# Residual sums as identity matmuls, statistics as ScalarE sums, and a last stage that adds four parts behind

## The reference, cut to what matters

```
def _forward(x, ...):
    m  = _mamba(x, ...)                        # 512 channels, 16 states: a scan over the tokens
    h  = _layernorm(m + x, ln0_g, ln0_b)       # residual sum 1 ("h")
    q  = gelu(_l2norm(h @ q_w.T + q_b))
    k  = _l2norm(h @ k_w.T + k_b)
    G  = (_l2norm(q @ w_g * D ** -0.5, 1) * q).sum(1)
    hs = G[:, None, :] * k @ proj_w.T + proj_b
    hs = hs * _layernorm(h, lni_g, lni_b) @ fl_w.T + fl_b      # h's second norm ("hi")
    h2 = _layernorm(hs + h, ln1_g, ln1_b)      # residual sum 2 ("s")
    f  = gelu(h2 @ d1_w.T + d1_b) @ d2_w.T + d2_b
    return _layernorm(f + h2, ln2_g, ln2_b)    # residual sum 3 ("f"); its result is "o"

x = x + _layernorm(_forward(_layernorm(x)))    # o's norm
x = x + _layernorm(_experts(_layernorm(x)))    # the sum of the last stage
```

## Time and profile before

| | |
|---|---|
| three runs | 6304.99, 6323.98, 6331.19 us; median 6323.98 us |
| profiled execution | 6312.81 us, of which the span from first to last instruction is 6311.1 us |
| granted TensorE clock, mean | 0.926 of full speed |
| busy share of the span | PE 85%, DVE 80%, POOL 71%, ACT 58% |
| end of the attention phase's last scan | about 5475 us, then its tail to about 5665 us |
| expert phase | to about 6176 us |
| last stage | 6176 us to the end |

### The profile page before, as it was taken

How to read it: one execution, slowest core, us unless ns; L and a number is a source line. 1 busy time by engine, 2 the same in 40 slices (tenths; PEclk the granted TensorE clock), 3 DMA queues, 4 the chain that set the end, 5 groups by cost and what they waited for, 6 DMA issues and landing times. The chain is left out here.

```text
span 6311.1 us, 71449 instructions
## 1 busy us (share of the span) xinstructions
PE 5337.9 (85%) x16896; PEld 2976.5 (47%) x16896; DVE 5058.4 (80%) x6651; ACT 3688.4 (58%) x6370; POOL 4465.4 (71%) x3013
## 2 busy tenths in 40 slices
PE   5788888888888888988888888888898888749990
PEld 2344444444444444444444444444444444436660
DVE  5888989998889899898888999988898898612224
ACT  5566666666666666666666666666666665321114
POOL 3677777777777777777777777777777777523446
PEclk8899999999999999999999999999999999869995
DMA  7876666666666666666666666666665666405556
GB/s 223 277 244 228 227 229 228 235 226 219 223 220 226 222 222 223 220 226 222 224 217 227 218 218 216 220 212 218 218 219 201 222 220 213 145 27 119 122 109 220
DMA packets 486058, 1316.23 MB, mean 209 GB/s; under 512 B 54687, under 2 KB 194976, under 8 KB 485552
## 3 DMA queue, kind: packets, MB, share of 16 engines
q1 hardware_dynamic: 441424, 1242.65, 58.4%
q0 software_dynamic: 30720, 34.17, 3.0%
q10 hardware_dynamic: 13408, 34.08, 1.4%
HBM read 1189.94 MB, written 138.02 MB: 210 GB/s over the span
## 5 line engine op out<-in xcount | busy, mean ns | idle before, releaser
L529 POOL TENSOR_TENSOR st<-st,C_rows 128x1024 f32<-128x1024 f32 x1024 | 2478.7, 2427 | 520.1 <-DVE st L1111 509.9
L1111 DVE TENSOR_TENSOR_SCAN st<-dA,drive 128x1024 f32<-128x1024 f32 x1024 | 2338.9, 2284 | 242.4 <-PE y L920 117.1
L920 PE MATMUL y<-st,ident 128*128 128x512 f32 x4096 | 1974.4, 620 | 171.6 <-POOL st L529 168.4
L745 ACT ACTIVATE dA<-delta,a_neg 128x511 f32<-128x511 f32 x2048 | 1367.8, 712 | 706.8 <-DVE st L1111 698.1
L920 PEld LDWEIGHTS y<-st,ident 128*128 128x128 f32 x4096 | 793.3, 199 | 1193.7 <-issue 865.4
L1084 DVE TENSOR_TENSOR drive<-du,B_rows 128x1024 f32<-128x1024 f32 x1024 | 1260.2, 1231 | 107.5 <-DVE du L1079 20.7
L889 PE MATMUL pre_bank<-e_abs,in_w 128*128 128x512 f32 x1024 | 587.9, 715 | 86.2 <-DVE u L1061 78.1
L866 PE MATMUL post_bank<-d_w,gT 128*128 128x256 f32 x2048 | 464.2, 383 | 30.3 <-issue 29.6
L617 POOL DMA_INDIRECT expert_in<-tb,idx x256 | 271.8, 1062 | 264.0 <-DVE idx L1266 190.7
L866 PEld LDWEIGHTS post_bank<-d_w,gT 128*128 128x128 f32 x2048 | 391.9, 192 | 129.0 <-issue 77.1
L1427 POOL DMA_INDIRECT token_rows<-O,dest_i x128 | 198.1, 1547 | 307.2 <-DVE O L1474 219.9
(11 more groups left out here) (210 smaller groups left out, 8048.9 us busy)
## 6 DMA issues: line engine op xcount, KB each, us to landing
B_rows<-bc_rows SPq DMA_DIRECT2D x1024, 512.0 KB
C_rows<-bc_rows SPq DMA_DIRECT2D x1024, 512.0 KB, 5.1
expert_in<-zeros ACTq DMA_DIRECT2D x22, 768.0 KB, 5.5
X<-expert_in SPq DMA_DIRECT2D x32, 528.0 KB, 4.8
xin<-in_x SPq DMA_DIRECT2D x32, 512.0 KB, 6.9
xn_rows<-xin SPq DMA_DIRECT2D x32, 512.0 KB, 3.3
token_rows<-zeros SPq DMA_DIRECT2D x32, 512.0 KB, 7.4
h<-xn_rows SPq DMA_DIRECT2D x32, 512.0 KB, 7.8
```

What stands on the lines that cost most here:

```text
L529: pool.tensor_tensor(tile[:, :, :], tile[:, :, :], bc[1][k % ROWS[1]][:, :, :], ALU.mult)\
L745: return act.activation(dA[k % 2][:, j, 1:L], delta[par][:, c, 1:L], ACT.Exp, scale=a_neg[:, c, n:n + 1])
L920: last = pe.matmul(Y[:, :], ident[:, :], st[k % RING][:, j, :], start=False, stop=pair == CU - 1 and j == 1)
L1111: dve.tensor_tensor_scan(st[k % RING][:, :, :].rearrange("p a l -> p (a l)"), dA[k % 2][:, :, :].rearrange("p a l -> p (a l)"), DR[:, :, : ...
```

## The change

1. **Sums on TensorE.** For `h`, `s` and `f` the summand comes into the PSUM accumulation as one more matmul for each tile, with the identity (`residual` in `token_major`, and the same in `late`). That is 12 matmuls of 256 columns for each sequence. VectorE's statistics and ScalarE's normalisation now read the banks. `h` must therefore have landed before TensorE's first output projection, so its load moves to the end of the scan before (`load_h`).
2. **Statistics on ScalarE.** Those of `hi` and `o` become two accumulating passes of ScalarE each, in the manner of the input's norm. The number of GpSimd's small instructions stays.
3. **New places.** All `at` tuples are new, and more pieces have a place of their own, for instance each of the four Silu gates `g0` to `g3`. VectorE's two `delta` pieces go from slots 82 and 88 to the end of the scan (95), the last gate of the scan before from slot 2 to slot 0.
4. **The last stage** sums four turns behind instead of two, in SBUF, three of four parts on VectorE and one on GpSimd.

```diff
@@ SP
+            def load_h(b, par):
+                sp.wait_ge(*post_pe.at("fl", b - 1))
+                sp.wait_ge(xn_stored, 16 * (b + 1))
+                sp.dma_start(h[:, :, :], xn_v[par]).then_inc(xn_loaded, 16)
@@ ACT, pre
                 for c in range(KI):
-                    if c == 2:
+                    if c:
                         yield next(at)
                     act.wait_ge(*pre_pe.at(f"g{c}", b))
@@ ACT, post
+                act.wait_ge(*post_pool.at("h_b", b))
+                act.wait_ge(*post_act.at("q_sq", b))
+                sum_of(junk, h, sum_hi).then_inc(post_act.did("hi_sum"), 1)
+                yield next(at)
+                act.wait_ge(*post_pool.at("hi_m", b))
+                act.wait_ge(*post_act.at("hi_sum", b))
+                squares_of(junk, h, shift, sq_hi).then_inc(post_act.did("hi_sq"), 1)
@@ PE
+            def token_major(srcT, w, K, tile, banks=PB, residual=None):
+                dst = tiles_in(banks)[tile]
+                for c in range(K):
+                    last = pe.matmul(dst, srcT[:, c, tile * P:(tile + 1) * P], w[:, c, :], start=c == 0,
+                                     stop=residual is None and c == K - 1)
+                if residual is not None:
+                    last = pe.matmul(dst, ident[:, :], residual[:, tile, :], start=False, stop=True)
                 return last
...
+                    if tile == 0:
+                        pe.wait_ge(xn_loaded, 16 * (b + 1))
+                    token_major(u[par], out_w, KI, tile, RB, h).then_inc(post_pe.did(f"m{tile}"), 1)
@@ DVE, pre and gates
-                at = iter((20, 28, 33, 39, 82, 88, 95))
+                at = iter((23, 25, 28, 28, 29, 31, 32, 37, 95, 95, 95))
@@ DVE, post
-                dve.wait_ge(*post_pe.at("m1", b))
-                dve.wait_ge(xn_loaded, 16 * (b + 1))
-                for i in range(2):
-                    last = dve.tensor_tensor(h[:, 2 * i:2 * i + 2, :], RB[i][:, :].rearrange("p (a d) -> p a d", a=2),
-                                             h[:, 2 * i:2 * i + 2, :], ALU.add)
-                last.then_inc(post_dve.did("h_sum"), 1)
+                dve.wait_ge(*post_pe.at("m3", b))
+                yield from stats(post_dve, "h", tiles_in(RB), stat, mv, b, at)
...
-                dve.wait_ge(*post_pool.at("h_b", b))
-                stats(post_dve, "hi", tiles_of(h), stat, mv, b)
@@ DVE, late
-                dve.wait_ge(*late_dve.at("f_normed", b))
-                stats(late_dve, "o", tiles_of(s), stat_late, mv_late, b)
@@ last stage
-        H = 4
+        LAG = 4
...
+        def c_out(n):
+            return c_out_pool if n % 4 == 1 else c_out_dve
...
-            turns(dve, ((2, add), (0, stats)))
+            turns(dve, ((LAG, add), (0, stats)))
```

More of the change, by code:

```diff
@@ L942, in post @@
                 turn(h, PB).then_inc(post_pe.did("hT"), 1)
-                yield next(at)
-                pe.wait_ge(*post_act.at("hT", b))
-                token_major(F, q_w, KD).then_inc(post_pe.did("q"), 1)
+                for tile in range(TT):
+                    if tile % 2 == 0:
+                        yield next(at)
+                    if tile == 0:
+                        pe.wait_ge(*post_act.at("hT", b))
+                    last = token_major(F, q_w, KD, tile)
+                last.then_inc(post_pe.did("q"), 1)
                 yield next(at)
@@ L969, in post @@
                     .then_inc(post_pe.did("G"), 1)
-                yield next(at)
-                pe.wait_ge(*post_act.at("proj_g", b))
-                token_major(kT, proj_g, KD).then_inc(post_pe.did("hs"), 1)
+                for tile in range(TT):
+                    if tile % 2 == 0:
+                        yield next(at)
+                    if tile == 0:
+                        pe.wait_ge(*post_act.at("proj_g", b))
+                    last = token_major(kT, proj_g, KD, tile)
+                last.then_inc(post_pe.did("hs"), 1)
                 yield next(at)
@@ L975, in post @@
                 turn(tb, PB).then_inc(post_pe.did("tT"), 1)
-                yield next(at)
-                pe.wait_ge(*post_act.at("tT", b))
-                token_major(F, fl_w, KD).then_inc(post_pe.did("fl"), 1)
+                for tile in range(TT):
+                    if tile % 2 == 0:
+                        yield next(at)
+                    if tile == 0:
+                        pe.wait_ge(*post_act.at("tT", b))
+                        pe.wait_ge(*post_pool.at("h_fl", b))
+                    last = token_major(F, fl_w, KD, tile, PB, h)
+                last.then_inc(post_pe.did("fl"), 1)
                 yield next(at)
@@ L1602, in add @@
                     .then_inc(c_out_pool.did(n), 1)
[L1604 removed]
+            turns(pool, ((LAG, add), (0, scale_and_shift)))
         @block.scalar
```

212 lines of the change are left out of this document (113 added, 99 removed).

## The result

The changed kernel takes 6233.6 us (median of 5 runs, 6231.7 to 6237.5), the kernel before 6323.0 beside it (6305.0 to 6331.2). The ratio is 0.9866, with a 95% interval of 0.9851 to 0.9882: 1.3% faster, where 3.2% (6120 us) was forecast. The profiled execution has a span of 6232.0 us against 6311.1.

What follows compares the result with a forecast made beforehand. VectorE sets the pace, TensorE next with almost no room. 232 - 15 - 15 - 40 + 20 + 18 - 7 = 193 us off 6312.8 gave 6120 us, own range 6065 to 6180, overall 6040 to 6240.

Steps and rivals of the forecast that it cites:

- part 3: TensorE's 12 identity matmuls a sequence: 5.3 us of work, priced between nothing (hidden) and 5.3, taken as 0.5, 15 us lost.
- the ring of four: In the scan, four `st` tiles let TensorE's `add` be late by steps; a reason for taking 0.5 us a sequence.
- part 6: New places in the scan: of the 3.7 us a sequence that `recur` waits for `add`, 0.65 won, 20 us.
- The first rival: TensorE becomes the bound: 12 of its 19.7 us idle cannot be filled, 167.2 us a sequence, 6228 us; chance 0.15.
- Parts 1 and 2: Residual sums (120 us) and statistics (112 us) leave VectorE: 232 us won, 7.5 us a sequence.
- Part 4: ScalarE gains two norms and five table loads, 110.7 to 124.6 us a sequence; priced at 0.5, 15 us lost.
- Part 5: At scan ends VectorE waits 2.4 us before the gate (start T + 8.9); mean 1.3 a sequence, 40 us lost.
- Parts 7 and 8: The last stage with sums four turns behind, 18 us won; the tail, one chain through all engines, 7 us lost.

Runs made afterwards that it cites:

- e4: The changed kernel with each of the 12 identity matmuls followed by one that adds zeros: 6389.6 us, ratio 1.0102 to the kernel before.
- e16: e13 with each identity matmul of the residual sums doubled by one of zeros: 6310.7 us, ratio 0.9987 to the kernel before.
- e13: The changed kernel with dummy matmuls in TensorE's two long waits, three before `cum` and four before `G`: 6159.1 us, ratio 0.9740 to the kernel before.
- e5: The changed kernel with the residual sum of `s` back on VectorE: 6329.6 us, ratio 1.0013 to the kernel before.
- e6: The changed kernel with all three residual sums back on VectorE: 6412.3 us, ratio 1.0145 to the kernel before.
- e11: The changed kernel with the statistics of `hi` and `o` back on VectorE: 6372.1 us, ratio 1.0086 to the kernel before.
- e3: The changed kernel with `delta` back in slots 82 and 88 and the steps that feed it earlier: 6373.3 us, ratio 1.0082 to the kernel before.
- e2: The changed kernel with GpSimd's eight indirect DMAs back in their earlier slots, six in one run: 6218.2 us, ratio 0.9832 to the kernel before.
- e8: The changed kernel with ScalarE's four Silu gates in two pairs and TensorE's `g1` at slot 40: 6237.3 us, ratio 0.9871 to the kernel before.
- e1: The kernel before with the changed last stage alone: 6304.5 us, ratio 0.9972 to the kernel before.
- e17: e13 with the sum of `f` back on VectorE: 6151.4 us, ratio 0.9739 to the kernel before.
- e7: The changed kernel with TensorE's `k`, `G` and `cum` moved behind its next `add`: 6194.3 us, ratio 0.9802 to the kernel before.
- e12: The changed kernel with the place edits of e2 and e7 together: 6271.5 us, ratio 0.9931 to the kernel before.
- e9: The changed kernel with dummy matmuls in TensorE's two long waits, five before `cum` and seven before `G`: 6156.6 us, ratio 0.9751 to the kernel before.

## Why the prediction was wrong

**The step that failed is part 3**, TensorE's gain of 5.3 us "near the hidden end" at 0.5 us a sequence. The work was sized well (0.59 us for an identity matmul's two instructions with their end, 0.43 from one start to the next). Its price was not: e4 and e16 put it at 5.0 and 4.9 us a sequence, near the upper bound that the part itself gave. At that price the part is 31 x 4.5 = 140 us dearer, more than the 114 us by which the scans missed. This carries a price over: e4 and e16 add a second 5.3 us to the changed kernel, and no run isolates the change's own. "It lies in TensorE's 19.7 us of idle time" took the idle time as a place to work in. But it was idle in front of results from VectorE and ScalarE, in one part of the sequence, while two of the three sums went into the part with almost no gap. That the ring of four would hold a late `add` back from VectorE was the other half of the argument; in e4 the delay reached VectorE not through the ring but at the statistics of `f`, where it stands for `d2`.

**How the miss divides is not shown.** Put back into the new order, the old work costs more than the forecast gave for its removal: three sums 179 us (parts 1 and 3: 105), the statistics 138 (parts 2 and 4: 97), and the last stage 18 by itself. With 335 us for the pieces and 89 for the whole, the new places have to cost something against the old, or the pieces don't add up. The places were part 6, at 20 us won. The slow stretch behind `dt` is one such cost, but the new places with the old work were not run.

**The first rival had the number, and half of the mechanism.** It gave 167.2 us a sequence and 6228 us; measured are 167.6 and 6234. Its sign, waits for `add` of over 4.5 us a sequence, is there with 4.9. It had a chance of 0.15. The 12 us that cannot be filled were a guess there; measured are 13.4: waits of 3.4, 4.1 and 1.4 us for VectorE, and about 1 us each at gates and norms. That the number came out so close is partly luck. The half clock, worth 75 us in e13, was not in it, and TensorE's load alone as the bound is refuted by e5, e6 and e11. What the runs support is a loop through both engines, in which TensorE's work is paid, and VectorE's too wherever TensorE waits for it.

**Parts 1 and 2.** The work did leave VectorE. What was not foreseen is the 4.9 us that contention gave back. The 2.2 us of `delta` lie where VectorE would wait for TensorE (e3) and did not cause the miss. For the 2.7 us of the product with `w_g`, which TensorE waits for before `G`, that stays open: e2 freed VectorE of only 1.0 us a sequence, and half of it came back. The test that the prediction set, VectorE 7.5 us less and the sequence less than 3.5, asked for a fall that did not happen (3.4) and so did not bite.

**Part 4.** ScalarE's load came as worked out (124.2). `recur`'s wait for decays doubled to 2.8 us a sequence. e8 took 5.3 us off ScalarE, but that wait stayed, and so did the time. What the part cost is not shown.

**Part 5.** The wait before the gate was to be 2.4 us with a product of over 4 us. The product takes 3.24, and VectorE waits before the gate mainly at every second scan end (23.9 us in the window, 1.0 a sequence). The part let GpSimd's last product pace the gate. In e3, with no `delta` beside that product, the gate is later still, 11.6 us behind T, the start of the last `recur`, and stands for TensorE's own queue. In the changed kernel it starts at T + 8.8 at one scan end (2555.13 - 2546.37), near the T + 8.9 of the part, but by luck.

**Part 6** expected 20 us won from waits for `add`; they rose by 1.2 us a sequence. How much of that is TensorE's load and how much the places is not shown.

**Parts 7 and 8** hold: 18 us forecast, 15.8 between the traces and 18 in e1; 7 us lost forecast, 4.6 measured. In the last stage the window that answers to the earlier trace rows is

```profile
6130.00:6210.00 80.00, 0.00 (x0) 0.00 (x0) 64.29 (x211) 48.66 (x94) 69.74 (x100) 0.50 0.82 296
```

with GpSimd busy for 69.74 of 80 us (59.09 before) and a turn of about 3.1 to 3.5 us where VectorE adds:

```profile
6130.52 1.40 DVE L1604 BATCH_NORM_STATS2 c_stat<-rows 128x6 f32<-128x256 f32 x4
...
6133.97 1.39 DVE L1604 BATCH_NORM_STATS2 c_stat<-rows 128x6 f32<-128x256 f32 x4
...
6137.11 1.39 DVE L1604 BATCH_NORM_STATS2 c_stat<-rows 128x6 f32<-128x256 f32 x4
```

What stays open: a microsecond of VectorE's forecast work costs 2.4 in e5, 1.2 in e11 and next to nothing in e17. TensorE's waits in e5, e6 and e11 say that it is the place, but no run moves one instruction through the places alone. And the half clock was filled, not removed: a version that has useful work in the two waits wasn't found (e7 and e12 only moved them).

## What to carry to other kernels

Before work is moved to an engine "with room", cut one period of the trace into parts and look at that engine's busy share in the part where the new work will lie: here it was 98% there against 88% over the whole, and the price was 5 us a sequence instead of 0.5. In this loop of engines that each execute in order, the idle time of the second busiest was mostly waiting for the busiest. Load on either was paid, and a place in the order could cost more than the work. When contention is moved away from one instruction, look at what lies beside the other engine next: e2 shortened one instruction and lengthened another. Where TensorE stands in front of the same wait in every period and the granted clock behind it is 0.5, a few matmuls on zeros into a bank about to be overwritten tell in one run what its clock costs; here they gave 75 us, nearly as much as the whole change.

## What the runs showed of the hardware

- TensorE's clock: behind waits of 3.4 and 4.1 us the granted clock is 0.50 for some 4 and 9 us; with 2.7 and 3.5 us of dummy matmuls in them the window's mean is 0.98 instead of 0.94. It also falls without a wait, behind six matmuls with only 16 rows: in 22 of 24 sequences of the changed kernel the eight `add` matmuls behind them take over 5 us, in e13 in 18 of 23, 3.70 us in the others. Whether the 16 rows are the reason no run shows. From e9, timeline of PE, with a granted clock of 0.68 over the second row:

```profile
2472.03 3.02 PE L951 MATMUL pre_bank<-xd,dt_w 16*128 16x512 f32 x6
2474.98 5.40 PE L967 MATMUL y<-st,ident 128*128 128x512 f32 x8
```

- VectorE with two SBUF inputs and a tensor instruction of GpSimd exclude each other for whole instructions in these traces, however short the one is, and either can be the one that waits: 0.42 us became 3.25 and 0.18 became 2.02 on VectorE, 2.36 became 3.24 on GpSimd. Beside GpSimd's indirect DMAs the same product takes 0.41.
